# Five PSUM banks for VectorE's ring and three for ScalarE's, in a fused decoder layer

## What is computed

```python
q = _heads(x @ Wq + bq);  k = _heads(x @ Wk + bk);  v = _heads(x @ Wv + bv)
att = jnp.einsum('bhqd,bhkd->bhqk', q, k) * scale
att = jnp.where(causal[None, None], att, -jnp.inf)
y = jnp.einsum('bhqk,bhkd->bhqd', jax.nn.softmax(att, axis=-1), v)
qc = _heads(x @ Wcq + bcq); kc = _heads(cross_input @ Wck + bck); vc = _heads(cross_input @ Wcv + bcv)
attc = jnp.einsum('bhqd,bhkd->bhqk', qc, kc) * scale
y = y + jnp.einsum('bhqk,bhkd->bhqd', jax.nn.softmax(attc, axis=-1), vc)
return y.transpose(0, 2, 1, 3).reshape(x.shape[0], T, C) @ Wp + bp
```

## Time and profile before

| | us |
|---|---|
| median of 3 runs | 2710.1 (2708.05 to 2710.48) |
| the profiled execution's own time | 2708.37 |
| its span, first to last instruction | 2706.6 |
| TensorE matmul busy | 2457.8 (91%) |
| VectorE busy | 1907.8 (70%) |
| ScalarE busy | 1358.8 (50%) |

### The profile page before, as it was taken

How to read it: one execution, slowest core, us unless ns; L and a number is a source line. 1 busy time by engine, 2 the same in 40 slices (tenths; PEclk the granted TensorE clock), 3 DMA queues, 4 the chain that set the end, 5 groups by cost and what they waited for, 6 DMA issues and landing times.

```text
span 2706.6 us, 43627 instructions
## 1 busy us (share of the span) xinstructions
PE 2457.8 (91%) x13250; PEld 1153.0 (43%) x13250; DVE 1907.8 (70%) x5270; ACT 1358.8 (50%) x2937; POOL 192.9 (7%) x353
## 2 busy tenths in 40 slices
PE   5899988999889989899898998989988999879994
PEld 2344333544335433354334543345443444334442
DVE  6768466685767858588585885858767586665865
ACT  3635564355644547346472464824647246553550
POOL 2010000100011000110001100011000110000000
PEclk8999889998899988999899998999989999789996
DMA  5500033000430004200051000600015000240000
GB/s 136 97 9 1 1 71 71 9 2 1 92 66 1 2 9 99 50 2 1 10 110 39 2 2 17 120 21 2 1 38 103 8 1 1 55 86 1 1 1 16
DMA packets 284176, 91.54 MB, mean 34 GB/s; under 512 B 269344, under 2 KB 279712, under 8 KB 283936
## 3 DMA queue, kind: packets, MB, share of 16 engines
q1 hardware_dynamic: 283936, 88.60, 16.2%
HBM read 17.27 MB, written 4.19 MB: 8 GB/s over the span
## 4 chain that ended last, share of the span: by engine, by line
PE 79%; DVE 9%; ACT 6%; issue 4%; DMA 2%; POOL 0%; DVEq 0%; SPq 0%; ACTq 0%; POOLq 0%
PE bank L1316 18%; PE bank L1098 13%; PE bank L1364 12%; PE bank L1350 9%; PE bank L1209 4%; PE bank L1312 4%; PE bank L1347 4%; PE bank L1194 3%; PE bank L1202 3%; ACT work L551 2%; PE bank L1239 2%; ACT work L593 2%; DVE work L689 2%; PE bank L1137 2%; PE bank L1372 1%
## 5 line engine op out<-in xcount | busy, mean ns | idle before, releaser
L593 ACT ACTIVATE work<-bank 128x512 f32<-128x512 f32 (+3 forms) x1536 | 743.4, 555 | 642.7 <-PE bank L1350 297.5
L949 DVE TENSOR_REDUCE top_half<-bank 128x1 f32<-128x512 f32 x1024 | 625.8, 682 | 24.2 <-PE bank L1316 24.2
L1316 PE MATMUL bank<-k_c,q_c 32*128 32x512 f32 x2048 | 630.0, 638 | 0.0
L1350 PE MATMUL bank<-q_c,k_c 32*128 32x512 f32 x2048 | 585.6, 660 | 16.3 <-ACT work L593 15.8
L551 ACT ACTIVATE work<-work,neg 128x512 bf16<-128x512 bf16 x512 | 362.0, 711 | 27.8 <-DVE work L689 27.2
L1316 PEld LDWEIGHTS bank<-k_c,q_c 32*128 32x128 f32 x2048 | 272.9, 185 | 221.2 <-DVE top_half L949 142.8
L689 DVE TENSOR_SCALAR_CACHE_REDUCE work<-bank 128x512 bf16<-128x512 f32 x512 | 322.0, 686 | 64.0 <-PE bank L1194 63.7
L1364 PE MATMUL bank<-work,v_flat 128*32 128x512 f32 (+3 forms) x3072 | 337.9, 584 | 6.8 <-ACT work L593 6.6
L946 DVE CUSTOM_DVE_ANT_0 masked<-bank,mask_w 128x384 bf16<-128x384 f32 (+3 forms) x512 | 223.1, 488 | 109.2 <-PE bank L1312 105.2
L1350 PEld LDWEIGHTS bank<-q_c,k_c 32*128 32x128 f32 x2048 | 253.3, 188 | 105.6 <-ACT work L593 65.6
L1347 PE MATMUL bank<-q_s,k_s 32*128 32x512 f32 (+3 forms) x1024 | 266.4, 484 | 0.0
(11 more groups left out here) (195 smaller groups left out, 2386.4 us busy)
## 6 DMA issues: line engine op xcount, KB each, us to landing
xT_pad<-xT SPq DMA_DIRECT2D x16, 256.0 KB, 2.7
ctx_sb<-ctxT SPq DMA_DIRECT2D x8, 512.0 KB, 3.6
x_res<-x SPq DMA_DIRECT2D x8, 512.0 KB, 4.4
out<-k_s SPq DMA_DIRECT2D x8, 512.0 KB, 3.2
work<-work SPq DMA_TRANSPOSE x128, 4.3
qk_sb<-qkT SPq DMA_DIRECT2D x1, 512.0 KB, 4.7
wq_sb<-Wq SPq DMA_DIRECT2D x1, 512.0 KB, 6.4
wk_sb<-Wk SPq DMA_DIRECT2D x1, 512.0 KB, 6.9
```

The source lines that it names most:

```text
L593: nc.scalar.activation(pT[:, s % PT_SLOTS, g, q0:S], bank[:, RING + n % EXP_RING, 0:S - q0], ACT.Exp, scale=SCALE).then_inc(pT_ready, 1)
L949: nc.vector.tensor_reduce(top_half[:, i % 2, g, u // 2, u % 2:u % 2 + 1], scores, AX.X, ALU.max, negate=True).then_inc(slot_out, 1)
L1316: mm(dst, q_c[rows, i, P * t:P * (t + 1)], k_c[rows, i, S * half:S * (half + 1)], start=True, stop=True, tile_position=(GW * g, 0)).then_i ...
L1350: mm(dst, k_c[rows, i, P * u:P * (u + 1)], q_c[rows, i, :], start=True, stop=True, tile_position=(GW * g, 0)).then_inc(sT_mm, 1)
```

## The change

VectorE's ring gets banks 0 to 4, and ScalarE's ring banks 5 to 7. All that follows from this is done with it: a use waits for the use five places before it, a `scoresT` for the exponential three before it, a `unit` for the unit three before it. The two self value projections move from bank 7, which now belongs to the units, to bank 4, which belongs to the maxima; so TensorE waits for VectorE to have read both (`vj_evac`) ahead of the first `scores` instead of ahead of the fourth `unit`. The wait that stood at the second `unit` stands at the first. The number of uses of a batch is kept a multiple of the ring's length by one use that has no work (`pad`), counted by a semaphore increment of 2 in place of 1. VectorE's masked reduction waits also for the one four reductions before it, since both write the same `masked` buffer.

```diff
-    RING, EXP_RING = 4, 4
+    RING, EXP_RING = 5, 3
...
-    FFN_USES = 4
+    PAD = 1
+    FFN_USES = 4 + PAD
...
-            order += [("pv", ALL_STEPS // BURST - 1), ("o", CROSS, HG - 1)]
+            order += [("pv", ALL_STEPS // BURST - 1), ("o", CROSS, HG - 1)] + [("pad", i) for i in range(PAD if ffn else 0)]
...
-                    nc.vector.tensor_tensor(v_all[:, t:t + 2, :, 0:HD], bank[:, 7, :].rearrange("p (t h j) -> p t h j", t=2, h=H),
+                    nc.vector.tensor_tensor(v_all[:, t:t + 2, :, 0:HD], bank[:, 7 if i < CTX_PAIRS else 4, :].rearrange("p (t h j) -> p t h j", t=2, h=H),
...
+                            if m > 0:
+                                dve.wait_ge(slot_out, base + uses["max", m - 1, r] + 1)
...
-                                            rec[:, kind].unsqueeze(3).broadcast_to([P, NT, GH, HD]), ALU.mult).then_inc(slot_out, 1)
+                                            rec[:, kind].unsqueeze(3).broadcast_to([P, NT, GH, HD]), ALU.mult).then_inc(slot_out, filled)
...
-                        dst = bank[:, 7, D * half:D * (half + 1)]
+                        dst = bank[:, 7 if i < CTX_PAIRS else 4, D * half:D * (half + 1)]
...
-                    if u == 1 and ahead:
+                    if u == 0 and ahead:
                         pe.wait_ge(ex_evac, (b + 1) * EXTRAS + V_AT + 2)
-                    if u == 3:
-                        pe.wait_ge(vj_evac, (b + 1) * PAIRS)
...
+                pe.wait_ge(vj_evac, (b + 1) * PAIRS)
                 for m in range(LEAD):
```

More of the change, by code:

```diff
@@ L980, in finish @@
                     dve.wait_ge(rec_step, b * 2 * HG + n + 1)
+                    filled = 1 + (PAD if prev and n == 2 * HG - 1 else 0)
                     nc.vector.tensor_tensor(y if kind == SELF else y_tmp[:], o[:, :, :, 0:HD],
-                                            rec[:, kind].unsqueeze(3).broadcast_to([P, NT, GH, HD]), ALU.mult).then_inc(slot_out, 1)
+                                            rec[:, kind].unsqueeze(3).broadcast_to([P, NT, GH, HD]), ALU.mult).then_inc(slot_out, filled)
                     if kind == CROSS:
-                        dve.wait_ge(slot_out, base + use + 1)
+                        dve.wait_ge(slot_out, base + use + filled)
                         nc.vector.tensor_tensor(y, y, y_tmp[:], ALU.add).then_inc(y_done, 1)
@@ L1372, in o_transpose @@
                         last = nc.tensor.transpose(dst[:, P * t:P * (t + 1)], o_rows[:, kind, P * t:P * (t + 1)], ident[:])
-                    last.then_inc(slot_in, 1)
+                    last.then_inc(slot_in, 1 + (PAD if prev and kind == CROSS and i == HG - 1 else 0))
+                pe.wait_ge(vj_evac, (b + 1) * PAIRS)
                 for m in range(LEAD):
```

## The result

| | before | changed |
|---|---|---|
| median of the runs of this comparison, us | 2709.07 (4 runs) | 2865.91 (4 runs, 2860.83 to 2870.75) |
| ratio, 95% interval | | 1.0582 (1.0558 to 1.0606) |
| span of the profiled execution, us | 2706.6 | 2865.7 |
| mean granted TensorE clock in it | 0.927 | 0.900 |

The prediction said slower, but 2783 with a range to 2820. So the direction was right, and the loss was 157 us where 73 were forecast.

A forecast was written before the change was run, and what follows sets the result against it. TensorE was taken to bound the kernel, with ScalarE's three-bank ring setting a slower pace. Terms 0.25 - 1.6 + 3.65 + 7.1 gave +9.4 us for seven batches, +6.8 for batch 0: +72.6, so 2783 us, range 2745 to 2820.

The forecast's parts named there:

- The steps without maxima, +7.1 a batch: Steps 37 to 47: ScalarE's three-bank round trip of 1.80 us sets the pace, nothing covers it; +7.1 us a batch.
- 1.6 + 1.8 + 1.1: Batch 0's losses in us: two runs of eight (steps 37 to 40), steps 41 to 44, and steps 45 to 47.
- the clock falls more often: Rival: longer TensorE pauses bring more half clock in steps without maxima, 3.9 us a batch, 2814 us; beyond 2810, chance 0.13.
- Cross steps with maxima, +3.65: Steps 17 to 36: three banks delay each of five bursts by 0.73 us, +3.65 us a batch.
- a rival doubted: Rival, dense steps don't lose: fifth bank pays in cross steps, +0.65 for +3.65, total 2759 us; smaller losses had 0.10.
- Causal steps, -1.6: Causal steps: fifth bank lets TensorE run further ahead at four bursts, -0.4 us each, -1.6 a batch, between -2.4 and 0.
- Where the maxima begin, +0.25: Batch's first `scores`: moved wait for VectorE's reading of values +0.85 us, one reduction earlier afterwards -0.6, together +0.25.
- the edits at nothing: VectorE's added masked-reduction wait, the unused place and units waiting three back: claimed to cost no time.

The follow-up runs named there:

- three fillers: Unread matmuls behind three of each step's four `scoresT` from step 37 on, added to the changed kernel (2835.45 us) and to the kernel before (2730.72 us).
- the kernel with three and no fifth: Kernel before with three banks in ScalarE's ring, still four in VectorE's, bank 7 serving only the values: 2906.73 us, 1.0742.
- fillers in steps 37 to 40: Kernel before with unread matmuls behind three of each step's four `scoresT` in steps 37 to 40 alone: 2694.74 us, 0.9956.
- the two halves of the ring's cost: Two runs of the kernel before, `scoresT` waiting three exponentials back: only from step 37 on, 2831.45 us; only up to step 36, 2767.78 us.
- heavier `gather`: Kernel before with eight unread 128-row, 512-column bf16 matmuls among the small ones of `gather` in batches 1 to 7: 2711.37 us, 0.9994.

## Why the prediction was off

*The steps without maxima, +7.1 a batch: this step failed.* The term took it that the clock would keep the pattern that it had in the kernel before. It priced two runs of eight, steps 41 to 44 and the last twelve at the clock that the kernel before had shown there, and only step 44 at half. Measured was +16.4. Its mechanism held: the round trip was 1.81 us, 2.75 at half clock, and the loads came in threes. At full clock its size was somewhat too small: in batch 0, which has no feed-forward work, the terms add to 1.6 + 1.8 + 1.1 = +4.5, where 5.0 was measured with fillers in both kernels, and about 7 is the estimate without. In the other batches no pair at full clock throughout exists; the nearest is batch 1 of the changed kernel with three fillers against the kernel before, 48.7 against 40.1 with 11 and 10 us at half clock, +8.6, which contains the fillers' own cost, for a forecast of +7.1. What was missing is that with the longer pauses, 0.60 from load to load for 0.49, TensorE has half clock in more of these steps: 35.6 us a batch for 11.4. With 5 to 7 in batch 0 and at most 8.6 in seven batches, the ring takes at most about 8 of the 16.4, and the rest, at least some 8 a batch or 65 us in all, is the clock's.

*The rival "the clock falls more often", at 0.13, was this case*, in the right direction and with too small a size. It took one run of eight and one burst more at half clock, 3.9 us a batch. In batch 1 the time at half clock rose from 10 to 41 us, which is 70% of the stretch. That loads 0.60 us apart bring more half clock, no row had shown; the runs do: the clock is 0.65 in 649.00 to 707.40 for the 0.87 of the earlier trace rows, and with the pauses filled the half clock of these steps went from 35.6 to 11.5 us a batch. No row gave a size for it. What the prediction could have done was to take, as this rival's upper bound, all of the steps without maxima at half clock. It had the price, 0.32 more for each exponential: 44 of them are up to 14 us a batch, and 112 in all on top of 2783, so that the bound would have been about 2895.

*Cross steps with maxima, +3.65: right in batch 1, 9 us short over all.* Two loads of the changed kernel in step 20, and the burst behind it:

```profile
586.22 0.29 PEld L1352 LDWEIGHTS bank<-q_c,k_c 32*128 32x128 f32 x2 [0.68 <-ACT work L594]
587.27 0.16 PEld L1366 LDWEIGHTS bank<-work,v_flat 128*32 128x32 f32 x8 [0.76 <-DVE top_half L952]
```

The fourth load waits for ScalarE, 1.85 after the first at 584.37 (1.84 was worked out), and from the first `scoresT` at 576.28 to the burst it is 10.99 us, for a forecast of 10.96 and 10.23 before. The stretch is 3.6 longer. Over steps 16 to 36 batches 0, 6 and 7 lost 5.8 and the others 4.1; why is not shown. That the fifth bank gives nothing there, which a rival doubted, is shown: the kernel with three and no fifth takes the same 78.46.

*Causal steps, -1.6: the gain is smaller.* The mean is -0.9. In batch 1 it is -1.2, but there some 4 us at half clock (2 x 0.03 x 62.1) are gone. Where both kernels have the same clock, it is nothing. Batch 2 of the changed kernel, at 0.97:

```profile
863.70:925.80 62.10, 61.95 (x461) 35.14 (x460) 53.67 (x142) 27.86 (x68) 10.15 (x16) 0.97 0.01 2
```

The stretch of the earlier trace rows was 62.10 at 0.97, too, and in batch 0, where both kernels are at full clock, the causal part takes 61.1 for 60.7. Both halves of the term are in the waits of batch 1's causal stretch. Before:

```profile
DVE featA L961 <- PE bank L1364: 4.7, 3, 2.4
...
PEld bank L1347 <- ACT work L593: 1.0, 4, 0.2
```

Changed:

```profile
PEld bank L1349 <- ACT work L594: 4.5, 13, 0.6
DVE featA L964 <- PE bank L1366: 4.2, 3, 2.2
```

VectorE's waits for the end of a burst shrank by 0.5 in three, where the term took 0.4 for each of four, and TensorE's wait for exponentials grew from 1.0 to 4.5. The fifth bank does pay here, 2.4 us at full clock by the kernel with three and no fifth; and waiting three back cost 2.4 (59.4 for 57.0), by the experiment that had it in steps 0 to 36. The term let the fifth bank gain up to 2.4 and took 0.8 of it off for the ring of three, which cost all of it.

*Where the maxima begin, +0.25, and the edits at nothing.* The part between the batches went from 157.0 to 156.3, which follows its half clock, 30.0 to 28.3; a quarter of a us can't be told from it.

*The sum.* Forecast and measured, eight batches: steps without maxima 54 and 131, cross steps with maxima 29 and 38, causal steps -13 and -7. The forecast missed 84 us: 77 of them are in the first term, 9 and 6 in the other two, and the part between the batches gave 7 back (-5 measured, +2 forecast), which leaves 1 of rounding.

*What stays open.* Which batch keeps its clock and which doesn't, with the same program, isn't explained: three fillers gave 39.5, 48.7 and 56.4 us for these steps. That TensorE's pauses are what loses the clock is borne out by the changed kernel alone, where fillers cut the half clock from 35.6 to 11.5 us a batch; in the kernel before they left it at 11.5 and 11.9 for 11.4. It isn't shown why fillers in steps 37 to 40 help between the batches, nor why the two halves of the ring's cost keep more of the clock there than the whole.

## What to carry to other kernels

Compare a ring's round trip with its banks times the pace: here 1.80 us against four times 0.49 (hidden) and three times 0.49 (not). What the other ring gains by the bank then has to be judged with this ring already holding the engine back. When a change makes TensorE pause longer in a stretch whose clock already wavers, price the whole stretch at both clocks: here 0.87 became 0.65. A list of waits tells who is waited for, not what a bank is worth; one kernel with the bank taken away and not given tells it.

## What the runs showed of the hardware

- Loads of 32-row, 512-column float32 matmuls 0.60 us apart in place of 0.49 at full clock went with 35.6 us at half clock in place of 11.4 for each batch's steps without maxima, and with 34.7 when one wait was all that had been changed.
- A matmul that nobody needs behind each `scoresT` brought these steps to 11.5 us at half clock and the kernel from 2866 to 2808 us.
- One us at half clock cost a third to a half of a us in these steps where the program was the same: 7.7 us for 16 (changed kernel, three fillers), 7.1 for about 14 (heavier `gather`, 47.0 less 39.9), 2.6 for 8 (changed kernel, 58.3 less 55.7).
- Twelve such matmuls a batch made the kernel before 0.4% faster (0.9956, 0.9935 to 0.9977), with less half clock in batch 0, and between the batches, where none of them stands (24.9 us for 30.0).
